# Deform stage of a four-layer convolution kernel: bilinear sides summed by VectorE, and a gathered table of four images

## The chip, the cores and the metric

One core of one Trainium2 chip runs the whole program. The metric is the device time of one execution in microseconds; the median of the runs is given. Engines are named as in the profile: PE is TensorE (its weight loads are listed as PEld), DVE is VectorE, ACT is ScalarE, POOL is GpSimd and SP is SyncE, which only issues DMAs here.

## What is computed

A batch of 32 images of 64 channels and 56 x 56 pixels goes through four residual layers: a hyperbolic two-convolution block, a quantised block, a grouped sign-convolution block, and a deformable 3 x 3 convolution. The change lies in the last one. Cut to what matters:

```python
x = x + _L0_conv_ref(_gn(x), ...)      # stages a_ and b_ of the kernel
x = x + _L1_conv_ref(_gn(x), ...)      # stage c_
x = x + _L2_conv_ref(_gn(x), ...)      # stage d_
x = x + _L3_conv_ref(_gn(x), L3_conv_offset_w, L3_conv_deform_w)   # stage e_

# in the deformable layer, per pixel and tap (9 taps), at a learned fractional position:
p = corner(y0i, x0i, (1 - ly) * (1 - lx))
p = p + corner(y0i, x0i + 1, (1 - ly) * lx)
p = p + corner(y0i + 1, x0i, ly * (1 - lx))
p = p + corner(y0i + 1, x0i + 1, ly * lx)      # then a 64 x 64 matrix per tap
```

`corner` reads the image at integer positions given by data, zero outside of it. So each output pixel needs 9 taps x 4 corners x 64 channels, gathered.

## The kernel before

The stages run one after the other with a barrier between them. Images are worked in pairs (`PAIRS` = 16), 128 partitions holding two images of 64 channels.

**The table.** The deform stage (`deform_phase`) writes each normalised image into a table in DRAM, `k.table`, with `TY` x `TX` = 58 x 59 entries of `ENTRY` = 128 floats. An entry holds a pixel of the row and the one below it, so two neighbouring entries, 256 floats, are the four corners of a tap. The rim has to be zero: the first stage (`l0_conv_phase`, `first`) writes zeros to the table by DMAs from POOL (L496), one for each image of the table, while it computes.

**A tile** is 128 output pixels. There are 49 tiles in a pair (`PX_TILES`), worked in seven groups of seven (`GROUPS`, `SLOTS`); a group is the body `turn(p, group)`, written once for each engine and placed by `around`, which runs the groups of pair p and, between them, the preparations of pair p + 1: after group 0 `normalise`, after 1 `columns` (the table's rows, L1881), after 2 and 3 the offset convolution (`offsets`, L1893), after 4 `turn_offsets` (L1908) and `positions`; after group 6 comes `finish`. All engines follow this one order, each in its own instruction stream.

In a tile the work goes from engine to engine:

- POOL issues nine indirect DMAs (L1779, `gather(slot)`), one for each tap, into `g[:, slot]`. The slot must be free: POOL waits for `bank_done` of the tile that held it, and for `index_ready` from DVE.
- DVE copies the next nine indices (L2015), then multiplies all 2304 gathered values of a pixel with their corner weights in one instruction (L2032). The weights lie in a bank of PSUM, which ACT loads once per group (L1835) when the group before is wholly done.
- PE turns each tap over (pixels to the free side) by a matmul of `g` with the identity, and adds the left and the right side of the four corners in PSUM on the way: two calls per tap (L1922), 18 per tile.
- ACT copies the three banks to `corners` (L1845). PE multiplies with the deform weights, nine calls (L1932), into bank `OUT`, and ACT copies that to `big` (L1850).

A call of `matmul` on 32-bit floats becomes two pairs of weight load and matmul in the trace, so the two lines have 36 and 18 matmuls per tile there.

Of the kernel before, what the change touches and what calls it, by code (L numbers as in the profile page):

```python
# [16 lines left out]
F32 = mybir.dt.float32  # L17
BF16 = mybir.dt.bfloat16
U32 = mybir.dt.uint32
ALU = mybir.AluOpType  # L20
# [26 lines left out]
IMAGE_ENTRIES = TY * TX  # L47
PX_TILES = 2 * HW // P
# [349 lines left out]
def l0_conv_phase(nc, k, first):  # L398
# [8 lines left out]
    with ExitStack() as stack:  # L407
# [50 lines left out]
        with nc.Block() as block:  # L458
# [28 lines left out]
            def _(pool):  # L487
                for t in vpads:
                    pool.memset(t[:, :], 0.0).then_inc(zeroed, 1)
                if first:  # L490
# [1154 lines left out]
def deform_phase(nc, io, k):  # L1645
# [11 lines left out]
    STEPS = 15  # L1657
    with ExitStack() as stack:
# [10 lines left out]
        base, index_base = s.sb("base", [P, 2 * K3]), s.sb("index_base", [P, K3])  # L1669
        w_off, w_def = s.sb("w_off", [P, TAPS * C]), s.sb("w_def", [P, TAPS * C])  # L1670
# [5 lines left out]
        TURN, OUT, PREP, SMALL, WEIGHTS = (0, 1, 2), 3, (4, 5), 6, 7  # L1676
# [8 lines left out]
        (weighted, passed, bank_done, corners_ready, out_done, out_ready) = (  # L1685
            s.sem(n) for n in ("weighted", "passed", "bank_done", "corners_ready", "out_done", "out_ready"))
        (final_v, final_a, x3_used, switched, table_stored, w_loaded) = (
            s.sem(n) for n in ("final_v", "final_a", "x3_used", "switched", "table_stored", "w_loaded"))
        x3_back, stored = ([s.sem(f"{n}{b}") for b in range(2)] for n in ("x3_back", "stored"))
# [24 lines left out]
        with nc.Block() as block:  # L1714
            @block.sync
            def _(sp):
# [3 lines left out]
                def prepare(n):  # L1720
# [18 lines left out]
                    img = n * 2 if isinstance(n, int) else sp.snap(n * 2)  # L1739
# [55 lines left out]
            def _(act):  # L1795
# [35 lines left out]
                def turn(p, group, last=False):  # L1831

                    r = p * GROUPS + group
                    act.wait_ge(weighted, r * SLOTS)
# [28 lines left out]
            def _(pe):  # L1863
# [49 lines left out]
                def turn(p, group, last=False):  # L1913
                    for slot in range(SLOTS):
                        t = p * PX_TILES + group * SLOTS + slot
                        pe.wait_ge(corners_ready, t * 3)
                        pe.wait_ge(weighted, t + 1)
                        for tap in range(TAPS):
                            turned = ps[:, TURN[tap // 4], (tap % 4) * P:(tap % 4 + 1) * P]
                            for side in range(2):  # L1920
                                at_side = tap * CORNERS + side * 2 * C
                                mm = pe.matmul(turned, g[:, slot, at_side:at_side + 2 * C], k.ident[:, :],  # L1922
                                               start=(tap % 4 == 0 and side == 0),
                                               stop=(side == 1), skip_group_check=True)
                            if tap % 4 == 3 or tap == TAPS - 1:
                                mm.then_inc(bank_done, 1)
# [14 lines left out]
            def _(dve):  # L1941
                by_tap = lambda buffer, width: buffer.rearrange("p (n w) -> p n w", w=width)
                dve.wait_ge(const_in, 4 * 16)
# [295 lines left out]
```

## Time and profile before

| | |
|---|---|
| median of 3 runs | 17200.4 us (17161.67 to 17238.65) |
| the profiled execution | 17196.31 us, of which the span of the trace is 17194.7 us |
| PE busy | 11481.5 us (67%) |
| PE weight loads busy | 8617.8 us (50%) |
| POOL busy | 7498.9 us (44%), 7056 indirect DMAs among it |
| DVE busy | 4744.2 us (28%) |
| ACT busy | 3130.7 us (18%) |
| DMA queue of POOL's DMAs | 1020.12 MB, 22.5% of 16 engines' span |
| mean granted TensorE clock | 0.786 of full speed |

No engine is busy all the time, and the stages differ, so the shares of the whole span say little; what is read is the stretch of one stage, which wait ends last in it, and what each engine costs per tile. 784 tiles are worked in the deform stage.

### The profile page before, as it was taken

The numbers are of one execution on the slowest core, as the hardware profiler recorded it, in microseconds if no ns is written. First come the engines' busy times: TensorE is split into PE (matmuls) and PEld (weight loads), VectorE is DVE, ScalarE is ACT, GpSimd is POOL, SyncE is SP. The second block draws the span as 40 slices with busy tenths as digits, with TensorE's granted clock in tenths as the row PEclk, the third lists the DMA queues.
The fourth block names the chain that finished last, engine by engine and source line by source line (L and its number), as shares of the span: only waits on it lengthen the run. The fifth ranks groups of instructions, "written<-read, shape, count | busy, mean of one in ns | idle before, by whom it ended". The sixth has DMA issues, their size and how long they took to land.

```text
span 17194.7 us, 188269 instructions
## 1 busy us (share of the span) xinstructions
PE 11481.5 (67%) x72807; PEld 8617.8 (50%) x72807; DVE 4744.2 (28%) x6831; ACT 3130.7 (18%) x5214; POOL 7498.9 (44%) x7685
## 2 busy tenths in 40 slices
PE   3478788888566666656565657566666666576756
PEld 1133344448455555555555555555555555555555
DVE  3255465553111122121212121212121221212121
ACT  2133344432111111111111111111111111111111
POOL 0001222222455555554555454555455555555455
PEclk7689899999777777777787777777777777787777
DMA  6722111126323233332323232323232332323232
GB/s 103 97 75 83 57 56 56 54 85 184 95 75 99 78 94 85 91 92 77 92 80 92 77 95 78 102 75 103 71 96 77 98 93 81 92 80 97 78 88 75
DMA packets 556369, 1486.74 MB, mean 86 GB/s; under 512 B 174900, under 2 KB 280116, under 8 KB 526992
## 3 DMA queue, kind: packets, MB, share of 16 engines
q0 software_dynamic: 405760, 1020.12, 22.5%
q1 hardware_dynamic: 150032, 458.00, 8.9%
q8 instruction: 475, 7.78, 0.2%
q14 instruction: 102, 0.84, 0.0%
HBM read 1175.46 MB, written 301.96 MB: 86 GB/s over the span
## 4 chain that ended last, share of the span: by engine, by line
PE 43%; issue 18%; another core or an unknown queue 8%; DVE 4%; ACT 1%; DMA 1%; DVEq 0%; ACTq 0%; POOL 0%; SPq 0%
PE e_ps L1922 24%; PE e_ps L1932 11%; PE e_ps L1893 5%; PE e_ps L1908 2%; DVE e_g L2032 2%; PE e_ps L1881 1%; DVE e_sty L2038 1%; DMA out<-e_big 1%; DVE e_w_next L1999 0%; ACT e_corners L1845 0%; DVE e_big L2051 0%; ACT e_ps L1835 0%; DVE e_index_slots L2015 0%; DVE e_tmp L1988 0%
## 5 line engine op out<-in xcount | busy, mean ns | idle before, releaser
L1779 POOL DMA_INDIRECT e_g<-table_dram,e_index_slots x7056 | 6763.3, 959 | 6112.6 <-PE e_ps L1922 2686.4
L1922 PE MATMUL e_ps<-k_ident,e_g 128*128 128x128 f32 x28224 | 4620.1, 319 | 3029.3 <-issue 1805.0
L1922 PEld LDWEIGHTS e_ps<-k_ident,e_g 128*128 128x128 f32 x28224 | 4165.8, 228 | 3500.3 <-issue 2247.7
L1932 PE MATMUL e_ps<-e_corners,e_w_def 128*64 128x128 f32 x14112 | 2316.9, 322 | 1443.0 <-issue 1156.2
L1932 PEld LDWEIGHTS e_ps<-e_corners,e_w_def 128*64 128x64 f32 x14112 | 1901.1, 163 | 1746.6 <-issue 1313.3
L1845 ACT ACTIVATE e_corners<-e_ps 128x512 f32<-128x512 f32 (+1 forms) x2352 | 1119.5, 489 | 5139.6 <-remote 2459.4
L2032 DVE TENSOR_TENSOR e_g<-e_g,e_ps 128x2304 f32<-128x2304 f32 x784 | 1990.0, 2546 | 75.0 <-ACT e_ps L1835 75.0
L2015 DVE COPY e_index_slots<-e_index_now 128x9 uint32<-128x9 uint32 (+1 forms) x784 | 141.0, 181 | 6371.8 <-ACT e_ps L1835 6216.2
L1850 ACT ACTIVATE e_big<-e_ps 64x128 f32<-64x128 f32 (+1 forms) x784 | 212.6, 271 | 4907.3 <-remote 3595.4
L1893 PE MATMUL e_ps<-e_pad,e_w_off 128*64 128x448 f32 x2016 | 794.5, 551 | 32.0 <-issue 30.9
L1197 PE MATMUL c_ps<-c_spad,w_s 128*128 128x448 bf16 x3024 | 614.1, 364 | 7.6 <-ACT c_spad L1069 4.3
L1893 PEld LDWEIGHTS e_ps<-e_pad,e_w_off 128*64 128x64 f32 x2016 | 280.0, 140 | 527.9 <-issue 526.0
L612 PE MATMUL a_ps<-a_vpad,w_w 64*64 64x392 f32 x4608 | 481.7, 546 | 50.5 <-issue 49.6
L612 PE MATMUL b_ps<-b_vpad,w_w 64*64 64x392 f32 x4608 | 458.5, 523 | 25.0 <-issue 24.2
L171 PE MATMUL c_ps<-c_s,k_sel 128*28 128x224 f32 x2240 | 438.5, 355 | 38.3 <-ACT c_s L1012 17.8
L2038 DVE BATCH_NORM_STATS2 e_sty<-e_big 64x6 f32<-64x448 f32 x224 | 119.4, 603 | 1218.7 <-ACT e_big L1850 1143.0
L1197 PEld LDWEIGHTS c_ps<-c_spad,w_s 128*128 128x128 bf16 x3024 | 298.5, 100 | 312.9 <-issue 35.3
L1981 DVE TENSOR_TENSOR e_tmp<-e_ps,e_base 128x450 f32<-128x450 f32 (+1 forms) x32 | 19.8, 618 | 1545.6 <-PE e_ps L1908 1025.7
L1575 PE MATMUL d_ps<-d_spad,w_s 128*128 128x224 bf16 x4032 | 403.0, 261 | 27.0 <-ACT d_spad L1547 23.9
L1575 PEld LDWEIGHTS d_ps<-d_spad,w_s 128*128 128x128 bf16 x4032 | 386.5, 96 | 43.4 <-issue 24.0
L990 POOL TENSOR_TENSOR c_x1t<-c_s,c_xt 128x448 f32<-128x448 f32 x112 | 122.8, 1134 | 559.4 <-DVE c_s L1313 559.4
L1908 PE MATMUL e_ps<-k_ident,e_x3t 18*128 18x18 f32 (+1 forms) x1600 | 329.3, 359 | 55.1 <-issue 54.3
(434 smaller groups left out, 8007.8 us busy)
## 6 DMA issues: line engine op xcount, KB each, us to landing
e_g<-table_dram,e_index_slots POOLq DMA_INDIRECT x7056
table_dram<-a_zeros POOLq DMA_DIRECT2D x32, 1711.0 KB, 90.5
table_dram<-e_rt SPq DMA_DIRECT2D x32, 1624.0 KB
a_xt<-x_in SPq DMA_DIRECT2D x16, 1568.0 KB
v_dram<-a_vout SPq DMA_DIRECT2D x32, 784.0 KB, 8.7
b_xt<-v_dram SPq DMA_DIRECT2D x16, 1568.0 KB
v_dram<-b_vout SPq DMA_DIRECT2D x32, 784.0 KB, 7.3
c_v2t<-v_dram SPq DMA_DIRECT2D x16, 1568.0 KB
```

What stands on the lines that cost most here:

```text
L171: mm = pe.matmul(out, select[:, j, :], source[:, j * SCH:(j + 1) * SCH], start=(j == 0), stop=(j == NS - 1))
L612: mm = pe.matmul(ps[half * C:(half + 1) * C, CONV[2 * (r % 2) + img], 0:RC], w[img * C:(img + 1) * C, tap, :], tile_window(vpads[parity], ...
L1197: mm = pe.matmul(ps[:, CONV[j % 2], 0:CH], parts[n % 3][:, n // 3, :], window(spad[:, :], j, n // 3), start=(n == 0), stop=(n == 3 * TAPS ...
L1575: mm = pe.matmul(ps[:, n % 2, 0:SCH], parts[t % 3][:, t // 3, :], every_other_row(spad[b][:, :], j, t // 3), start=(t == 0), stop=(t == 3 ...
L1779: pool.indirect_dma_start(out=g[:, slot, tap * CORNERS:(tap + 1) * CORNERS], out_offset=None, in_=table, in_offset=bass.IndirectOffsetOnAx ...
L1845: act.activation(corners[:, taps[0]:taps[-1] + 1, :], ps[:, TURN[bank], 0:len(taps) * P].rearrange("p (k x) -> p k x", x=P), ACT.Copy).the ...
L1893: mm = pe.matmul(ps[0:C, PREP[j % 2], 0:CH], w_o[:, tap, :], window(pad[:, :], j, tap), start=(tap == 0), stop=(tap == TAPS - 1))
L1908: mm = pe.matmul(ps[to:to + hi - lo, PREP[half], col * 2 * TAPS:(col + 1) * 2 * TAPS], x3t[rows, lo:hi], k.ident[rows, rows], start=True, ...
L1922: mm = pe.matmul(turned, g[:, slot, at_side:at_side + 2 * C], k.ident[:, :], start=(tap % 4 == 0 and side == 0), stop=(side == 1), skip_gr ...
L1932: mm = pe.matmul(ps[0:C, OUT, 0:P], w_d[:, tap, :], corners[:, tap, :], start=(tap == 0), stop=(tap == TAPS - 1))
L2032: dve.tensor_tensor(tile, tile, w4.unsqueeze(2).broadcast_to([P, TAPS * 4, C]), ALU.mult).then_inc(weighted, 1)
L2038: ins = dve.bn_stats(sty[:, 6 * j:6 * j + 6], big[:, j * CH:(j + 1) * CH])
```

## The change

Two things are changed together.

1. DVE sums the two sides itself. In three batches of taps (4, 4 and 1) it multiplies the right sides into a PSUM bank, `HALF`, multiplies the left sides in place in `g`, waits for both, and adds the bank to `g`. PE then only transposes the sum, one call of `pe.transpose` per tap, batch by batch as DVE finishes them (`added`). The bank for `HALF` is the former `SMALL`; the few values of `SMALL` move to a bank of the preparations.
2. The table holds four images in place of 32; pair p uses half p % 2. The positions are moved between the halves with one more small DVE instruction and a `[128, 1]` buffer. The first stage fills four images with zeros, not 32.

```diff
+TABLE_IMAGES = 4
@@ l0_conv_phase
-                    for b in range(B):
+                    for b in range(TABLE_IMAGES):
                         pool.dma_start(k.table[b]..., zeros...).then_inc(filled, 16)
-                    pool.wait_ge(filled, 16 * B)
+                    pool.wait_ge(filled, 16 * TABLE_IMAGES)
@@ deform_phase, SP
-                    img = n * 2 if isinstance(n, int) else sp.snap(n * 2)
+                    img = n * 2 % TABLE_IMAGES if isinstance(n, int) else sp.snap((n % 2) * 2)
@@ deform_phase, PE
                         pe.wait_ge(corners_ready, t * 3)
-                        pe.wait_ge(weighted, t + 1)
                         for tap in range(TAPS):
-                            turned = ps[:, TURN[tap // 4], (tap % 4) * P:(tap % 4 + 1) * P]
-                            for side in range(2):
-                                at_side = tap * CORNERS + side * 2 * C
-                                mm = pe.matmul(turned, g[:, slot, at_side:at_side + 2 * C], k.ident[:, :],
-                                               start=(tap % 4 == 0 and side == 0),
-                                               stop=(side == 1), skip_group_check=True)
+                            if tap % 4 == 0:
+                                pe.wait_ge(added, t * 3 + (tap // 4 + 1))
+                            mm = pe.transpose(ps[:, TURN[tap // 4], (tap % 4) * P:(tap % 4 + 1) * P],
+                                              g[:, slot, tap * CORNERS:tap * CORNERS + 2 * C], k.ident[:, :])
@@ deform_phase, DVE, positions
-                    c.then(dve.scalar_tensor_tensor(index_next[:, :], flat, float(ENTRY), index_base[:, :],
-                                                    ALU.mult, ALU.add))
-                    c.then(dve.tensor_scalar(index_base[:, :], index_base[:, :],
-                                             float(2 * IMAGE_ENTRIES * ENTRY), None, ALU.add))
+                    c.then(dve.tensor_scalar(flat, flat, float(ENTRY), table_half[:, 0:1], ALU.mult, ALU.add))
+                    c.then(dve.tensor_tensor(index_next[:, :], flat, index_base[:, :], ALU.add))
+                    c.then(dve.tensor_scalar(table_half[:, :], table_half[:, :], -1.0,
+                                             float(2 * IMAGE_ENTRIES * ENTRY), ALU.mult, ALU.add))
@@ deform_phase, DVE, turn
-                        dve.tensor_tensor(tile, tile, w4.unsqueeze(2).broadcast_to([P, TAPS * 4, C]),
-                                          ALU.mult).then_inc(weighted, 1)
+                        for n, (lo, hi) in enumerate(BATCHES):
+                            left = sides[:, lo:hi, 0, :, :]
+                            half = ps[:, HALF, 0:(hi - lo) * 2 * C].rearrange("p (k n c) -> p k n c", n=2, c=C)
+                            need(dve, added, t * 3 + n)
+                            dve.tensor_tensor(half, sides[:, lo:hi, 1, :, :], spread(1), ALU.mult).then_inc(weighted, 1)
+                            dve.tensor_tensor(left, left, spread(0), ALU.mult).then_inc(weighted, 1)
+                            dve.wait_ge(weighted, t * 6 + (2 * n + 2))
+                            dve.tensor_tensor(left, left, half, ALU.add).then_inc(added, 1)
```

On PE, at the start of a group in the deform stage, one tile reads so before the change (each row is a call or a run of equal calls; `e_g` is the gathered tile, `e_ps` the PSUM banks, `k_ident` the identity):

```order
L1916 ISA
L1917 REGISTER_ALU
L1922 MATMUL e_ps<-k_ident,e_g 128x128 x18
L1929 REGISTER_ALU
L1932 MATMUL e_ps<-e_corners,e_w_def 64x128 x4
```

and so after it:

```order
L1921 ISA
L1924 REGISTER_ALU
L1925 MATMUL e_ps<-k_ident,e_g 128x128 x4
L1924 REGISTER_ALU
L1925 MATMUL e_ps<-k_ident,e_g 128x128 x4
L1924 REGISTER_ALU
L1925 MATMUL e_ps<-k_ident,e_g 128x128
L1934 MATMUL e_ps<-e_corners,e_w_def 64x128 x9
```

The 18 calls on the gathered tile became nine, in three runs with a wait value for each; the nine calls with the deform weights are the same.

On DVE, at the start of a group, two tiles read so before the change (the copy is that of the next indices):

```order
L2027 ISA
L2015 COPY e_index_slots<-e_index_now 128x9
L2032 TENSOR_TENSOR e_g<-e_g,e_ps 128x2304
L2015 COPY e_index_slots<-e_index_now 128x9
L2032 TENSOR_TENSOR e_g<-e_g,e_ps 128x2304
```

and the first two batches of one tile read so after it:

```order
L2019 COPY e_index_slots<-e_index_now 128x9
L63 ISA
L2044 TENSOR_TENSOR e_ps<-e_g,e_ps 128x512
L2045 TENSOR_TENSOR e_g<-e_g,e_ps 128x4x128
L2046 ISA
L2047 TENSOR_TENSOR e_g<-e_g,e_ps 128x4x128
L63 REGISTER_ALU
L2044 TENSOR_TENSOR e_ps<-e_g,e_ps 128x512
L2045 TENSOR_TENSOR e_g<-e_g,e_ps 128x4x128
L2046 REGISTER_ALU
L2047 TENSOR_TENSOR e_g<-e_g,e_ps 128x4x128
```

The third batch follows with three instructions on 128 elements. One instruction on 2304 elements became nine, six on 512 elements and three on 128, with a wait on DVE's own results before each first and each third of a batch.

## Rows read from the trace of the kernel before

**Rows 1.** Stretches: start:end, us, busy PE, PEld, DVE, ACT, POOL; PEclk, DMA share, GB/s

```profile
75.00:930.00 855.00, 371.83 (x3622) 151.73 (x3623) 236.96 (x525) 176.60 (x238) 44.01 (x31) 0.70 0.72 100
930.00:1174.00 244.00, 229.98 (x2560) 94.02 (x2562) 152.10 (x338) 113.74 (x158) 0.00 (x0) 0.96 0.30 79
...
4382.00:17128.00 12746.00, 8108.61 (x47128) 6844.46 (x47129) 2647.37 (x2368) 1634.52 (x3641) 6762.81 (x7056) 0.76 0.31 88
```

**Rows 2.** Convolution matmuls of the first stage, L612, 288 per pair, by stretch

```profile
75.00:930.00 855.00, 295.15 (x2680) 103.62 (x2680) 0.70 0.72 100
930.00:1174.00 244.00, 185.89 (x1924) 67.10 (x1928) 0.96 0.30 79
```

**Rows 3.** The zero fill, L496: issues, first and last start, time to landing

```profile
L496 POOL DMA_DIRECT2D table_dram<-a_zeros x32: 1395/2934/4472, 73.3 to 712.3; - x32
...
DMA to landing us min/median/max: 5.4/90.5/219.9
```

**Rows 4.** Waits for the input of the first stage, 0 to 1200 us

```profile
DVE a_st L706 <- DMA a_xt<-x_in: 452.0, 11, 104.3
```

**Rows 5.** POOL's waits, 4382 to 17128 us: total, times, longest

```profile
POOL e_g L1779 <- PE e_ps L1922: 2686.4, 261, 41.5
...
POOL e_g L1779 <- DVE e_index_slots L2015: 867.6, 38, 129.4
POOL e_g L1779 <- remote: 607.9, 373, 7.1
```

**Rows 6.** Groups of instructions, 4382 to 17128 us: busy, mean ns, idle before

```profile
L1779 POOL DMA_INDIRECT e_g<-table_dram,e_index_slots x7056 | 6763.3, 959 | 6112.6 <-PE e_ps L1922 2686.4 <-issue 1950.6 <-DVE e_index_slots L2015 867.6
...
L2032 DVE TENSOR_TENSOR e_g<-e_g,e_ps 128x2304 f32<-128x2304 f32 x781 | 1982.6, 2546 | 75.0 <-ACT e_ps L1835 75.0
```

**Rows 7.** PE in order of time, one group: start, us, last bracket idle before

```profile
9084.95 4.29 PE L1922 MATMUL e_ps<-k_ident,e_g 128*128 128x128 f32 x36
...
9098.70 0.27 PE L1922 MATMUL e_ps<-k_ident,e_g 128*128 128x128 f32 x1 [0.35 <-issue]
9100.09 0.27 PE L1922 MATMUL e_ps<-k_ident,e_g 128*128 128x128 f32 x1 [1.13 <-issue]
...
9109.20 2.28 PE L1922 MATMUL e_ps<-k_ident,e_g 128*128 128x128 f32 x9 [0.32 <-issue]
...
9177.54 6.83 PE L1922 MATMUL e_ps<-k_ident,e_g 128*128 128x128 f32 x36 [11.70 <-issue]
```

**Rows 8.** POOL in order of time, same group

```profile
9083.82 0.95 POOL L1779 DMA_INDIRECT e_g<-table_dram,e_index_slots  x1 [33.07 <-PE e_ps L1922]
...
9105.13 0.95 POOL L1779 DMA_INDIRECT e_g<-table_dram,e_index_slots  x1 [0.30 <-issue]
9112.37 0.95 POOL L1779 DMA_INDIRECT e_g<-table_dram,e_index_slots  x1 [6.30 <-PE e_ps L1922]
```

**Rows 9.** PE in order of time, last group, after the last gather

```profile
17157.00 4.29 PE L1922 MATMUL e_ps<-k_ident,e_g 128*128 128x128 f32 x36
17161.22 2.18 PE L1932 MATMUL e_ps<-e_corners,e_w_def 128*64 128x128 f32 x18
```

**Rows 10.** PE's waits for the first tile of a group, 4382 to 17128 us

```profile
PE e_ps L1922 <- DVE e_g L2032: 1208.1, 108, 43.8
```

**Rows 11.** PE's matmuls of the preparations, 4382 to 17128 us

```profile
L1893 PE MATMUL e_ps<-e_pad,e_w_off 128*64 128x448 f32 x1890 | 746.9, 552 | 31.3 <-issue 30.9
L1908 PE MATMUL e_ps<-k_ident,e_x3t 18*128 18x18 f32 (+1 forms) x1500 | 309.5, 359 | 54.5 <-issue 54.3
...
L1881 PE MATMUL e_ps<-k_ident,e_pad 128*56 128x128 f32 x1680 | 252.7, 322 | 95.3 <-ACT e_rt L1813 53.0 <-issue 42.2
```

**Rows 12.** DVE multiplications on 392 elements with a PSUM input, 75 to 1174 us

```profile
L778 DVE TENSOR_TENSOR a_vpad<-a_ps,a_tile 128x392 f32<-128x392 f32 x128 | 66.6, 562 | 104.7 <-PE a_ps L145 104.3
```

**Rows 13.** A transposition and a matmul, one call each, in the first stage

```profile
L300 PE MATMUL z_ps<-k_ident,z_t x1: 369/369/369, 29.4 to 29.4; 128*1 128x128 f32 x1
L303 PE MATMUL z_ps<-z_max_one,z_one_row x2: 348/358/369, 30.4 to 30.6; 1*128 1x1 f32 x2
```

More of the change, by code:

```diff
@@ L1656, in deform_phase @@
     OFF_ROWS = 32 + 2 * TAPS
-    STEPS = 15
+    STEPS = 16
     with ExitStack() as stack:
@@ L1669, in deform_phase @@
         base, index_base = s.sb("base", [P, 2 * K3]), s.sb("index_base", [P, K3])
+        table_half = s.sb("table_half", [P, 1])
         w_off, w_def = s.sb("w_off", [P, TAPS * C]), s.sb("w_def", [P, TAPS * C])
@@ L1675, in deform_phase @@
         ps = s.ps("ps", [P, 8, 512])
-        TURN, OUT, PREP, SMALL, WEIGHTS = (0, 1, 2), 3, (4, 5), 6, 7
+        TURN, OUT, PREP, HALF, WEIGHTS = (0, 1, 2), 3, (4, 5), 6, 7
+        SMALL = PREP[1]
+        BATCHES = ((0, 4), (4, 8), (8, TAPS))
         padv = pad[:, :].rearrange("p (y x) -> p y x", x=PW)
@@ L1684, in deform_phase @@
                                "coord_step", "index_ready"))
-        (weighted, passed, bank_done, corners_ready, out_done, out_ready) = (
-            s.sem(n) for n in ("weighted", "passed", "bank_done", "corners_ready", "out_done", "out_ready"))
+        (weighted, added, passed, bank_done, corners_ready, out_done, out_ready) = (
+            s.sem(n) for n in ("weighted", "added", "passed", "bank_done", "corners_ready", "out_done", "out_ready"))
         (final_v, final_a, x3_used, switched, table_stored, w_loaded) = (
             s.sem(n) for n in ("final_v", "final_a", "x3_used", "switched", "table_stored", "w_loaded"))
+        half_ready = s.sem("half_ready")
         x3_back, stored = ([s.sem(f"{n}{b}") for b in range(2)] for n in ("x3_back", "stored"))
@@ L1833, in turn @@
                     r = p * GROUPS + group
-                    act.wait_ge(weighted, r * SLOTS)
+                    act.wait_ge(weighted, r * (SLOTS * 6))
                     act.activation(ps[:, WEIGHTS, 0:SLOTS * TAPS * 4],
@@ L1942, in _ @@
                 by_tap = lambda buffer, width: buffer.rearrange("p (n w) -> p n w", w=width)
+                dve.memset(table_half[:, :], 0.0).then_inc(half_ready, 1)
+                dve.wait_ge(half_ready, 1)
                 dve.wait_ge(const_in, 4 * 16)
@@ L2026, in turn @@
                     for slot in range(SLOTS):
+                        t = r * SLOTS + slot
                         dve.wait_ge(gathered[slot], r * (16 * TAPS) + 16 * TAPS)
@@ L2029, in turn @@
                             issue(slot, group * GK + (GK + slot * TAPS))
-                        tile = g[:, slot, :].rearrange("p (n c) -> p n c", c=C)
-                        w4 = ps[:, WEIGHTS, slot * TAPS * 4:(slot + 1) * TAPS * 4]
-                        dve.tensor_tensor(tile, tile, w4.unsqueeze(2).broadcast_to([P, TAPS * 4, C]),
-                                          ALU.mult).then_inc(weighted, 1)
+                        sides = g[:, slot, :].rearrange("p (k s n c) -> p k s n c", s=2, n=2, c=C)
+                        w4 = ps[:, WEIGHTS, slot * TAPS * 4:(slot + 1) * TAPS * 4].rearrange(
+                            "p (k s n) -> p k s n", s=2, n=2)
+                        for n, (lo, hi) in enumerate(BATCHES):
+                            left = sides[:, lo:hi, 0, :, :]
+                            half = ps[:, HALF, 0:(hi - lo) * 2 * C].rearrange("p (k n c) -> p k n c", n=2, c=C)
+                            spread = lambda side: w4[:, lo:hi, side, :].unsqueeze(3).broadcast_to([P, hi - lo, 2, C])
+                            need(dve, added, t * 3 + n)
[3 more added lines that the diff above has]
+                            dve.tensor_tensor(left, left, half, ALU.add).then_inc(added, 1)
                 def finish(p):
```

2 lines of the change are left out of this document (1 added, 1 removed).

## Prediction

> **What bounds the kernel now.** I read the stretches first, then the waits, then PE and POOL in order of time. The deform stage gathers from 4382 to 17128 us [rows 1]: 12,746 us for 16 pairs, 797 us each, or 113.8 us for each of 112 groups. No engine fills it: PE is busy 8109 us, POOL 6763, DVE 2647. POOL needs 0.959 us for an indirect DMA and about 0.305 between two (1950.6 us over 6384 gaps) [rows 6], 11.4 us a tile and 79.7 us a group. The other 34 us of a group POOL waits, mostly for PE to free a slot [rows 5].
>
> Why is PE late? After the last gather a tile costs it 4.29 us on the gathered tile and 2.18 on the deform weights, end to end 6.3 us [rows 9], so seven tiles would take 44 us. While gathers flow it looks different. POOL starts at 9083.82, PE still runs 36 matmuls in 4.29 us at 9084.95, but from 9098.70, 15 us into the flow, matmuls come singly, 1.4 us apart at first; no semaphore is named ("issue"). POOL ends its last gather at 9106.08 and idles 6.3 us, for this very tile; at 9109.20, 3 us later, PE runs again nine at once [rows 7, 8]. I call this a hold. POOL's own stops release PE, and PE's holds bring about the stops. So a group costs POOL's 79.7 us, plus the stops, plus the gap before the next group's first tile, since ACT may load the weights only when PE is through.
>
> The gap is 11.7 us where no preparation lies in it (before 9177.54) [rows 7]. Five boundaries of each pair carry one or the finish: PE's waits for the first multiplication, 1208.1 us [rows 10], and its matmuls of the preparations, 746.9 + 309.5 + 252.7 us [rows 11], are 2517 us over about 79 such boundaries, 31.9 us each.
>
> In the first stage DVE waited 452 us for its input [rows 4] while the 32 fills ran from 73.3 us on, the last issued at 712.3 and up to 219.9 us in flight [rows 3]. Until 930 us there are 2680 convolution matmuls, 9.3 pairs at 92 us; after it 1924 in 244 us, 6.7 pairs at 36.5 us; the DMA share falls from 0.72 to 0.30 [rows 1, 2].
>
> **The change, part by part.** *Fill.* Four of 32 transfers remain, about 855 x 4/32 = 107 us. In those I leave the disturbed pace, 1.2 pairs; the other 8.1 pairs cost 36.5 us each, 297 us. 855 becomes 404, a gain of 451; I take 440, since the first pair has to be loaded and filled in anyway. Bounds: 390 (two more pairs disturbed) to 455.
>
> *Table of four.* A pair still gathers from two images and writes two. Half p % 2 is rewritten by the preparations of pair p + 2, which run a whole pair after its gathers. No wait is added; the small DVE instruction more per pair is well under 1 us, nothing. If addresses within 7 MB or 55 MB mattered, the gathers' landing would show it; POOL does not wait for that, and I take zero.
>
> *DVE per tile.* 2304 elements take 2546 ns [rows 6], 392 take 562 [rows 12]: 1.04 ns an element and 155 ns fixed. So 512 elements take 687 ns and 128 take 288. Six and three are 4.98 us; with the index copy and a small allowance for nine starts with waits, which no row prices (0.3 us), 5.5 us against 2.6. No row shows DVE writing PSUM; if that costs another fixed part each, three times 0.155 makes 6.0, and below nothing speaks for less than 5.0. I take 5.5. Seven tiles are 39 us, under POOL's 80, and DVE does not wait for PE within a group: hidden, unless the holds end.
>
> *PE per tile.* A transposition is one matmul in the trace, another 32-bit call two [rows 13], so the tile goes from 36 + 18 matmuls to 9 + 18, at full speed from 6.3 us to about 3.2 (27 x 0.117), and with the wait for ACT's copies still below DVE's 5.5. PE follows DVE at 5.5 us a tile where nothing holds it.
>
> *The new group, step by step*, with time 0 at PE's first transposition. Slots 0, 1, 2 come free at 6, 11.5 and 17 us, and POOL gathers from 6 on. At 21 us, 15 into the flow, PE is held, with tile 3 half done. In the hold it did nine matmuls in 10.5 us [rows 7], so about 26 in 30 us at best, so by the time POOL has filled slots 0 to 3, at 6 + 4 x 11.4 = 51.6, it has brought through tile 3 but not tile 4's transpositions. POOL stops; 3 us later PE is free, at 56 slot 4 is, POOL resumes, and PE has 15 us again, in which it ends tiles 4, 5 and 6: at 68. Before, the same end lay near 89: the group whose second tile began at 9084.95, the first some 8 us earlier, ended at 9177.54 - 11.70 = 9165.8 [rows 7]. With a gap of 31.9 the next group begins at 99.9. With a short gap POOL is still busy with slots 5 and 6 until 56 + 3 x 11.4 = 90, PE is held again at 71, and the group lasts about 90. A pair is 5 x 99.9 + 2 x 90 = 680 us against 797; 16 pairs gain 1,872.
>
> *Sum.* 17,196 - 440 - 1,872 = 14,884 for the profiled execution's own 17,196; the median stands 4 us above that, which changes nothing. Forecast 14,880. Its own range is 14,300 to 15,600: the group's 68 us may be 62 to 74 (one tile of PE more or fewer before a hold, 112 x 6 = 670).
>
> **Rivals.**
>
> *A. The holds mostly vanish.* For it: they may come from something that PE has half as much of now, such as its instruction stream. Then PE follows DVE, POOL is the bound, and the gaps of 32 us are hidden, because POOL has seven slots (80 us) to fill before it needs the first. 4382 - 440 + 112 x 79.7 + 66 = 12,930 at the least; with loop passes, some holds and the finish, 13,100 to 14,200, say 13,600. Against it: the end of the hold follows POOL's stop, not PE's own progress [rows 7, 8]. Chance 0.27.
>
> A page of the Trainium skill offers such a mechanism: "Runtime: NRT & Kernel Launch", on instruction fetch, says that each engine's stream is refilled by DMA in blocks of 16 KiB (256 instructions), mostly hidden. No row here ties a hold to a block; if one did, half the matmuls would mean half the holds, and A's time.
>
> *B. The holds get longer.* POOL now has more freed slots in front of it when PE is held, so if PE does nearly nothing in a hold, tile 3 waits too and the group ends near 80: 112 x 12 = 1,340 less gain, 16,200. Chance 0.14; between 15,600 and 16,770, where only the fill's 440 would be left.
>
> *C. PE runs at half clock.* The mean was 0.76 [rows 1]; with half the matmuls it may fall to 1.2 GHz for good. 36 matmuls took 6.83 us at 9177.54 and 4.29 at 9084.95 [rows 7], so 0.19 us each and not 0.12; 27 are 5.1 us, with ACT's copies some 6.3 a tile. Each group is then some 5 us longer: 112 x 5 = 560, 15,440. Chance 0.10.
>
> A rule that speaks for C: "TensorE: Matmul & The Clock Gate", part 4, in the Trainium skill, says that transpositions do not count as activity for the clock. No row here shows a run of them.
>
> *D. Slower: DVE is held like PE.* DVE now has ten instructions a tile where it had two, and no row shows DVE working long within a flow of gathers. If each took 1.4 us, as PE's did from 9098.70 on, a tile would take 14 us, seven 98, and with the mean gap of about 25 a group 123: 861 us a pair, +1,020 - 440, 17,780. It decides from 13.5 us a tile on. Against it: POOL's and ACT's instructions keep their pace in the flow (POOL's 0.95 us [rows 8]). Chance 0.05.
>
> *E. Only the fill counts,* POOL and PE settle at the old rhythm: 16,760. Chance 0.04. The forecast has 0.40.
>
> **How the numbers follow.** A change of under 0.5% (86 us) can't be told from none here. Only D and a failed fill lie above: slower 0.05, within 0.01, faster 0.94. The range leaves out the fast end of A (0.06), the slow end of B, E and D (0.14 together): 13,250 to 16,150.
>
> **What the profile will show.** Fill: 4 transfers, DVE's wait for its input under 80 us, the first stage ending near 740 in place of 1174. DVE: nine instructions per tile at 687 and 288 ns; a PSUM write shows in the first of each batch. PE: 9 + 18 matmuls per tile; the line on the gathered tile from 28,224 to 7,056. POOL: 7056 DMAs at 0.959 us, its waits for PE from 2686 us to about 1,000. Holds: singles of the transpositions, mostly in tile 3, ended 3 us after POOL stops. If no singles are left and POOL never waits, A holds. If DVE's instructions stand apart with nothing waited for, D. The forecast is wrong if the 15 us that PE has in a flow depend on something that the change moves, DVE's activity above all.

## The result, and the profile after

The changed kernel took 16286.15 us (median of 4 runs, 16262.03 to 16311.95), the kernel before 17218.46 (4 runs beside it): ratio 0.9464, 95% interval 0.9435 to 0.9492. Faster, but by 932 us and not by the 2,320 forecast, and outside the range. The profiled execution took 16288.56 us, its span is 16286.9 us.

Stretches of the changed kernel, to compare with [rows 1] and [rows 2]: start:end, us, busy time of PE, PEld, DVE, ACT, POOL (instructions), then PEclk, DMA share, GB/s. First the first stage, then the deform stage.

```profile
75.00:719.00 644.00, 566.07 (x6180) 232.91 (x6184) 386.34 (x865) 290.11 (x395) 4.95 (x4) 0.93 0.33 86
3930.00:16220.00 12290.00, 5106.96 (x26109) 3958.54 (x26109) 4371.97 (x8603) 1556.74 (x3638) 6748.50 (x7056) 0.65 0.32 91
```

The fill of the table with zeros did what was forecast. The first stage ends at 719 us and not at 1174, a gain of 455 us (forecast 440). DVE's wait for its input fell from 452 us [rows 4] to 44.6, and four transfers stand where 32 stood [rows 3]:

```profile
DVE a_st L707 <- DMA a_xt<-x_in: 44.6, 4, 21.8
```

```profile
L497 POOL DMA_DIRECT2D table_dram<-a_zeros x4: 1628/2110/2734, 74.0 to 77.2; - x4
```

The deform stage gained as little: its gathers span 12,290 us in place of 12,746, 768 us a pair for 797, where 680 was forecast. Groups of instructions in it (busy us, mean ns, idle before them and what ended it), against [rows 6]:

```profile
L1784 POOL DMA_INDIRECT e_g<-table_dram,e_index_slots x7056 | 6748.5, 956 | 5670.3 <-PE e_ps L1925 2502.9 <-issue 2039.2 <-remote 951.6
L1934 PE MATMUL e_ps<-e_corners,e_w_def 128*64 128x128 f32 x13986 | 2515.5, 353 | 4618.9 <-ACT e_corners L1850 2998.2 <-issue 1590.0
...
L2044 DVE TENSOR_TENSOR e_ps<-e_g,e_ps 128x512 f32<-128x512 f32 (+1 forms) x2331 | 1314.6, 564 | 179.4 <-DVE e_g L2047 96.8 <-issue 25.0 <-remote 5.2
L2047 DVE TENSOR_TENSOR e_g<-e_g,e_ps 128x512 f32<-128x512 f32 (+1 forms) x2331 | 1291.2, 554 | 372.5 <-remote 162.2 <-DVE e_g L2045 82.7 <-issue 53.4
L2045 DVE TENSOR_TENSOR e_g<-e_g,e_ps 128x512 f32<-128x512 f32 (+1 forms) x2331 | 1273.5, 546 | 0.0
L1925 PE MATMUL e_ps<-k_ident,e_g 128*128 128x128 f32 x6993 | 1241.6, 325 | 1879.8 <-DVE e_g L2047 1771.0 <-issue 106.5
```

DVE's nine instructions are as priced, 0.68 to 0.70 us and 0.28 to 0.29, 4.9 us a tile (forecast 5.5), and the one that writes PSUM (L2044) costs no more than the other two. PE's line on the gathered tile is a quarter of what it was. But POOL still waits 2,503 us for PE, hardly less than the 2,686 of [rows 5], and its waits for something without a named releaser ("remote") rose from 608 to 952.

What PE is late with is seen in order of time (start, us; in brackets the idle time before and its releaser). POOL here begins to gather at 9001.9:

```profile
9006.08 2.18 PE L1934 MATMUL e_ps<-e_corners,e_w_def 128*64 128x128 f32 x18
...
9008.19 0.66 PE L1925 MATMUL e_ps<-k_ident,e_g 128*128 128x128 f32 x4
...
9010.37 0.33 PE L1925 MATMUL e_ps<-k_ident,e_g 128*128 128x128 f32 x1 [0.19 <-issue]
...
9021.88 0.94 POOL L1784 DMA_INDIRECT e_g<-table_dram,e_index_slots  x1 [0.30 <-issue]
9023.12 0.95 POOL L1784 DMA_INDIRECT e_g<-table_dram,e_index_slots  x1 [0.30 <-issue]
9027.31 0.27 ACT L1855 ACTIVATE e_big<-e_ps 64x128 f32<-64x128 f32 x1 [20.62 <-remote]
9027.49 1.23 ACT L1850 ACTIVATE e_corners<-e_ps 128x512 f32<-128x512 f32 x3
9028.12 2.18 PE L1934 MATMUL e_ps<-e_corners,e_w_def 128*64 128x128 f32 x9 [17.42 <-ACT e_corners L1850]
9028.32 0.94 POOL L1784 DMA_INDIRECT e_g<-table_dram,e_index_slots  x1 [4.25 <-remote]
```

PE ends its matmuls with the deform weights of one tile at 9008.3 by its record, and the next tile's transpositions at 9010.7. ACT, which waits for just these, starts at 9027.31. Between lies POOL's flow; its last gather ends at 9024.07. The semaphore events of the trace say why. An instruction tells the others that it is done by an increment of a semaphore. PE's four increments (the tile's end and the three banks) arrive together, from 9027.29 to 9027.45, up to 19 us after the matmuls that carry them. DVE worked on through these 17 us at its full pace, though in each batch it waits for increments of its own; those of them that are on record come 0.01 us after their instruction. **In this stretch PE is not slow by its records; its signals come late.** (The start of a matmul is recorded, its end is modelled, so what is seen is that it started in time and that its increment came late.)

I set every increment after 5000 us that is on record against the last instruction of its engine that carries it and had ended, by my own count. `bank_done` tells that a bank of transpositions is done, `out_done` that a tile's last matmul is. Share of PE's increments that come over 2 us late, and the delay that nine in ten stay under:

```
              bank_done        out_done
before      41%,  5.8 us     32%, 15.4 us
after       46%, 16.8 us     60%, 20.1 us
```

Of the increments on record that DVE and ACT give for a tile at most 4% of any semaphore are late. Most signals that come late have no releaser left beside them, so the chain that ended last puts 36% down to an unknown source:

```profile
another core or an unknown queue 36%; PE 19%; issue 12%; DVE 7%; ACT 2%; DMA 1%; ACTq 0%; DVEq 0%; SPq 0%
```

**Not every increment is on record.** After 5000 us the trace of the changed kernel holds 68% of the increments that PE, DVE and ACT give for a tile, and 19,938 of the 112,896 that the landings of the gathers give (7,056 gathers with 16 each); the trace of the kernel before holds 84%, and 30,597. So the shares above are shares of what was recorded. That DVE is not held doesn't rest on them: L2047 waits for DVE's own two increments, and all its idle time is 372.5 us in 2,331 instructions, the longest single wait 3.0 us.

**PE's matmuls come late too, but elsewhere.** Within a tile's run of 36 matmuls on the gathered tile the kernel before waits for nothing. Its trace still has 2,097 steps there of over 0.6 us from one start to the next, where 0.11 is usual, in 199 of the 784 tiles, 2,309 us together beyond it; those of [rows 7] are some of them. In the changed kernel the runs on the gathered tile have none, but the preparations' long runs (L1898 and L1913) have 295 of over 0.5 us beyond the usual step, 478 us together.

### The profile page after: what moved, and what is told of

Its sections match the earlier page's. It is cut to its first block, busy times and chain, and to the rows that moved or that the text cites. A ratio compares the mean times of both kernels' runs of the same rounds, so it can differ in the third digit from the quotient of the medians.

```text
span 16286.9 us, 156056 instructions
## 1 busy us (share of the span) xinstructions
PE 8435.4 (52%) x51639; PEld 5705.0 (35%) x51639; DVE 6489.5 (40%) x13120; ACT 3052.6 (19%) x5214; POOL 7443.3 (46%) x7657
## 4 chain that ended last, share of the span: by engine, by line
another core or an unknown queue 36%; PE 19%; issue 12%; DVE 7%; ACT 2%; DMA 1%; ACTq 0%; DVEq 0%; SPq 0%
PE e_ps L1934 7%; PE e_ps L1898 5%; PE e_ps L1925 2%; PE e_ps L1913 2%; DVE e_g L2045 2%; ACT e_corners L1850 1%; PE e_ps L1886 1%; DVE e_g L2047 1%; DVE e_sty L2052 1%; DMA out<-e_big 1%; DVE e_x3t L1958 1%; DVE e_big L2065 0%; DVE e_w_next L2003 0%; DVE e_x3t L1962 0%
## 5 line engine op out<-in xcount | busy, mean ns | idle before, releaser
L1934 PE MATMUL e_ps<-e_corners,e_w_def 128*64 128x128 f32 x14112 | 2532.7, 352 | 4619.1 <-ACT e_corners L1850 2998.2
L1934 PEld LDWEIGHTS e_ps<-e_corners,e_w_def 128*64 128x64 f32 x14112 | 2215.9, 184 | 4879.8 <-ACT e_corners L1850 3137.4
L1925 PE MATMUL e_ps<-k_ident,e_g 128*128 128x128 f32 x7056 | 1253.4, 325 | 1911.7 <-DVE e_g L2047 1803.0
L1925 PEld LDWEIGHTS e_ps<-k_ident,e_g 128*128 128x128 f32 x7056 | 939.4, 165 | 2223.7 <-DVE e_g L2047 1880.7
L1850 ACT ACTIVATE e_corners<-e_ps 128x512 f32<-128x512 f32 (+1 forms) x2352 | 1041.0, 489 | 2610.4 <-remote 1314.3
L2047 DVE TENSOR_TENSOR e_g<-e_g,e_ps 128x512 f32<-128x512 f32 (+1 forms) x2352 | 1302.8, 554 | 373.3 <-remote 162.2
L2044 DVE TENSOR_TENSOR e_ps<-e_g,e_ps 128x512 f32<-128x512 f32 (+1 forms) x2352 | 1326.4, 564 | 242.9 <-DVE e_g L2047 96.8
L2045 DVE TENSOR_TENSOR e_g<-e_g,e_ps 128x512 f32<-128x512 f32 (+1 forms) x2352 | 1285.0, 546 | 0.0
L1898 PE MATMUL e_ps<-e_pad,e_w_off 128*64 128x448 f32 x2016 | 908.4, 598 | 234.7 <-issue 230.9
L1898 PEld LDWEIGHTS e_ps<-e_pad,e_w_off 128*64 128x64 f32 x2016 | 297.2, 148 | 827.8 <-issue 821.3
L1913 PE MATMUL e_ps<-k_ident,e_x3t 18*128 18x18 f32 (+1 forms) x1600 | 324.3, 344 | 218.1 <-issue 217.3
```

The lines of the kernel that those rows point to most:

```text
L1850: act.activation(corners[:, taps[0]:taps[-1] + 1, :], ps[:, TURN[bank], 0:len(taps) * P].rearrange("p (k x) -> p k x", x=P), ACT.Copy).the ...
L1898: mm = pe.matmul(ps[0:C, PREP[j % 2], 0:CH], w_o[:, tap, :], window(pad[:, :], j, tap), start=(tap == 0), stop=(tap == TAPS - 1))
L1913: mm = pe.matmul(ps[to:to + hi - lo, PREP[half], col * 2 * TAPS:(col + 1) * 2 * TAPS], x3t[rows, lo:hi], k.ident[rows, rows], start=True, ...
L1925: mm = pe.transpose(ps[:, TURN[tap // 4], (tap % 4) * P:(tap % 4 + 1) * P], g[:, slot, tap * CORNERS:tap * CORNERS + 2 * C], k.ident[:, :])
L1934: mm = pe.matmul(ps[0:C, OUT, 0:P], w_d[:, tap, :], corners[:, tap, :], start=(tap == 0), stop=(tap == TAPS - 1))
L2044: dve.tensor_tensor(half, sides[:, lo:hi, 1, :, :], spread(1), ALU.mult).then_inc(weighted, 1)
```

## Experiments

The theory to test, **T**: PE's semaphore increments are held back while POOL's gathers flow at their full rate, and come when the flow pauses. I call a stretch in which they are held back a hold. Rivals: the holds are PE's own (its instruction supply, the pattern of its work), or they go by the bytes that move.

Each set of runs was made on one chip, with the kernel before run in it too. This came to matter: **the same kernel before took 17,180 and 17,224 us in two sets and 13,430, 13,418 and 13,445 us in three**, within 1% inside each set. I call them sets with and without holds; the first comparison (17,218 us) was one with holds. The chip on record has the number 11 in one set with holds and 13 in two without, but number 0 both in a set without holds and, half an hour later, in one with them. If the number names the same chip, the holds are no fixed property of a chip.

**Without gathers** (set with holds). All 7,056 are left out; `g` is zeroed once.

```diff
-                    for tap in range(TAPS):
-                        pool.indirect_dma_start(...).then_inc(gathered[slot], 16)
+                    pool.nop().then_inc(gathered[slot], 16 * TAPS)
```

> The changed kernel with all 7,056 gathers left out (the corner buffers are zeroed once), everything else as it is. Theory 1, TensorE's semaphore signals are held back by the flow of gathers: no hold is left, signals later than 2 us after their matmul fall from 46 and 60% to under 10%, and the stage is bound by VectorE's 4.9 us a tile (35 us a group) and the preparations, some 370 us a pair in place of 774, so about 9,800 us. Rival, the holds are TensorE's own (its instruction supply, or the pattern of its work): they stay, a group stays near 70 us and more, over 560 us a pair, 12,900 us or more.

Measured 10,286 us, 396 us a pair. Of PE's increments 0.3% at most are over 2 us late. The chain that ended last is DVE's now:

```profile
DVE 32%; PE 15%; issue 13%; DMA 2%; ACT 1%; DVEq 0%; ACTq 0%; SPq 0%
```

PE runs the same matmuls in the same order, so its own stream alone doesn't cause the holds. Nor does a supply slowed by the gathers fit: the DMA packets that bring instructions took at most 1.5 us each after 5000 us in the changed kernel with holds, and 1.6 without. T stands. This trace, of a set with holds, also has every increment on record, and no gap in PE's runs.

**Half the bytes** (with holds): only the left 128 floats of each row are gathered, the right side stays zero.

```diff
-                            out=g[:, slot, tap * CORNERS:(tap + 1) * CORNERS], ...
+                            out=g[:, slot, tap * CORNERS:tap * CORNERS + 2 * C], ...
```

> The changed kernel with gathers that bring only the left 128 of the 256 floats of each row, as many gathers and rows as before. What is left out is the right side, which is summed from a buffer zeroed once. If the hold goes by the bytes in flight, it vanishes or shrinks to less than half and the pair falls from 774 to some 600 us, about 13,500 us. If it goes by the number of descriptors (or is TensorE's own), the pair stays at 774 us, 16,290 us within 200.

Measured 16,239 us, ratio to before 0.9452 (0.9407 to 0.9496), as the changed kernel's 0.9464. POOL's instruction is as long, its wait for PE the same (2,458 for 2,503 us), late increments 48 and 59%:

```profile
L1788 POOL DMA_INDIRECT e_g<-table_dram,e_index_slots x7056 | 6755.5, 957 | 5612.7 <-PE e_ps L1929 2457.5
```

Not bytes: what is left is the number of gathers, of their rows or of their increments (16 for each landing) per time. No run separates these.

**Spaced gathers** (with holds): a memset of 256 bytes a partition behind each gather.

```diff
                         ).then_inc(gathered[slot], 16)
+                        pool.memset(pace[:, tap * 256:(tap + 1) * 256], 0).then_inc(paced, 1)
...
+                        pool.wait_ge(paced, r * GK + slot * TAPS)
                         pause(pool, index_ready, r * SLOTS + (slot + 1), passed)
```

> The changed kernel with a small memset of some 0.28 us on GpSimd behind each gather, so that they start every 1.55 us or so and not every 1.25. Theory 1, holds come of gathers at the full rate: they vanish or become rare, GpSimd's group is 63 x 1.55 = 98 us and sets the pace, 700 to 730 us a pair, 15,100 to 15,600 us. Rival, holds don't depend on the rate: they stay as long, and GpSimd's 18 us more a group come on top, 17,000 us or more.

Measured 14,919 us, ratio 0.8684 (0.8657 to 0.8710), under the range expected, since gathers start 1.447 us apart and not 1.55, and 2.17 between tiles (the wait for the last memset). POOL now does more and the kernel is 1,370 us faster than the changed one. Of the increments on record (88%) 0.3% at most are late, POOL's waits for PE fell from 2,503 us to

```profile
POOL e_g L1786 <- PE e_ps L1931: 1.6, 10, 0.2
```

and the chain that ended last is POOL's:

```profile
POOL 59%; issue 12%; PE 2%; DVE 1%; POOLq 1%; DMA 0%; ACT 0%; DVEq 0%; SPq 0%; ACTq 0%
```

**A pause at each tile** (with holds): POOL waits for the tile's gathers to land.

```diff
                         gather(slot)
+                        pool.wait_ge(gathered[slot], r * (16 * TAPS) + 16 * TAPS)
```

> The changed kernel in which GpSimd, behind the nine gathers of a tile, waits until they have landed before it goes on to the next tile: a pause of some 2 us every 11.3 us. Theory 1, a pause in the flow releases what TensorE has signalled: each tile's signals come within one tile, PE is late by at most some 13 us, GpSimd's group is 80 + 7 x 2 = 94 us and sets the pace, some 670 to 700 us a pair, 14,600 to 15,100 us. Rival, the holds are not of the flow: the pauses only come on top of the stops, 16,500 to 17,500 us.

Measured 15,246 us, ratio 0.8879 (0.8851 to 0.8908), above the range expected. Gathers are 1.25 us apart within a tile and 3.68 us between tiles, one pause longer than I had put in. Late increments: 4% (`bank_done`) and 20% (`out_done`, 99 in 100 of them within 5.8 us). So a hold begins within one tile of gathers and such a pause ends most of them.

**Shorter gaps.** One memset a tile in place of nine, and a memset of 16 in place of 256 behind each gather. Both were first run in sets without holds:

```diff
+                        if tap % 9 == 8:
                             pool.memset(pace[:, tap * 256:(tap + 1) * 256], 0).then_inc(paced, 1)
```

> The changed kernel with one memset of 256 columns (0.33 us, as in the paced kernel) behind each ninth gather only, once a tile. If a gap of this length lets out what TensorE has signalled, signals come within a tile (late by at most 11 us), GpSimd's group is 80 + 2 = 82 us and the pair some 590 to 640 us, 13,300 to 14,000 us. If it is the mean rate that counts, the rate is nearly unchanged, holds stay, and the time is 16,250 to 16,500 us.

> The changed kernel with a shorter memset (16 in place of 256 columns, some 0.12 us) on GpSimd behind each gather, so that they start every 1.4 us or so: 63 x 1.4 = 88 us a group, and a hold of TensorE's signals is then a matter of whether this is slow enough. If any slowing or any gap between gathers is enough, no hold, some 630 to 650 us a pair and 13,900 to 14,300 us. If the rate must fall to something near the 1.6 us of the paced kernel, holds are back for some or all of the time: 15,500 us or more.

They took 13,738 and 13,565 us, where before took 13,430: slower than before (ratios 1.0235 and 1.0109), with no signal held. A repeat of the first,

> The changed kernel with one memset of 0.33 us and the wait for the last one between tiles, so gathers start every 1.25 us within a tile and once after 2.2 us between tiles; where no signal was held it took 13,738 us, 612 us a pair. Theory: one such gap a tile lets out what TensorE has signalled, so that on a chip with holds too the time is 13,700 to 14,300 us. Rival, the mean rate counts or the gap must be near the 3.6 us of the kernel that waits for landing (709 us a pair there): 15,000 to 16,400 us.

gave 13,733 where before took 13,418. The missing holds look like the memsets' doing until the time of the kernel before in the same set is seen: they are missing there too. Then with holds:

> The kernel with one memset a tile again, for a chip on which the kernel before takes 17,200 us (twice it was run where before takes 13,430 us, and took 13,735). If the one gap of 2.2 us between the gathers of two tiles lets the signals out, 13,700 to 14,300 us. If the rate within a tile (1.25 us) starts a hold that so short a gap doesn't end, 15,000 to 16,400 us.

> The kernel with the short memset behind each gather again, for a chip on which before takes 17,200 us (13,565 us where it takes 13,430). Its gathers start every 1.26 us within a tile, as without memsets, and 1.96 us apart between tiles. If what ends a hold is time without a gather, this gap is the shortest of the three and it is at or above the kernel with one memset a tile: 15,500 to 16,400 us. If work of another kind between gathers on GpSimd is enough, 13,600 to 14,000 us.

Measured 15,845 and 15,973 us (ratios 0.9207 and 0.9278): 52 to 61% of increments late, and POOL still waits 1,755 and 1,916 us for PE (2,503 in the changed kernel). The short memset fits into the 0.30 us between two gathers; they stay 1.257 us apart within a tile, so work between them doesn't end the holds; nor does a gap of 2.2 us once a tile.

**Between 1.25 and 1.45 us** (the first with holds, the second without), memsets of 160 and 128:

> The changed kernel with a memset of 160 columns behind each gather: gathers some 1.35 us apart, between the 1.26 us of the short memset and the 1.45 us of the long one, with which no signal was held. GpSimd alone would set 90 us a group, some 635 us a pair, 14,050 to 14,200 us on either kind of chip, if 1.35 us is slow enough. If it isn't, 15,500 us or more on a chip with holds.

> The changed kernel with a memset of 128 columns behind each gather: gathers some 1.33 us apart, between 1.26 us (holds to 15 us and more, 15,973 us) and 1.36 us (holds to 5 us, 14,335 us). If the hold grows steadily as the interval shrinks, holds of 5 to 10 us and a time set by GpSimd still, 14,100 to 14,300 us. If there is an edge between the two, GpSimd stops again and it is over 14,500 us.

The first: 14,335 us, ratio to before 0.8328 (0.8297 to 0.8358), the fastest of all with holds and 12% under the changed kernel. Gathers are 1.363 us apart; 37% of PE's increments are late, but 99 in 100 come within 6.6 us, and POOL's waits for PE are 2 us in all. The second took 14,173 us at 1.340 us apart; where it ran no signal is ever held, so it says nothing of the limit.

In one table (intervals in us, pairs and the share of late increments among those on record, from the traces, by my own count):

```
with holds             gathers apart   between   late bank_/out_done  us a pair   us
changed kernel              1.251        1.25+        46% / 60%          774    16,286
16 behind each              1.257        1.96+        52% / 61%          757    15,973
256, once a tile            1.251        2.2+         56% / 56%          746    15,845
wait for landing            1.250        3.7           4% / 20%          709    15,246
256 behind each             1.447        2.17          0% / 0%           686    14,919
160 behind each             1.363        2.08         37% / 37%, short   649    14,335
without holds: changed      1.251        1.25          0% / 0%           564    12,969
```

**What differs between the sets in the traces** is how much of the increments they hold. Of the 112,896 of the gathers' landings, the eight traces of gathering kernels with holds have 17 to 69% (changed kernel 18%, 16 behind each 17%, once a tile 22%, 160 behind each 35%, 256 behind each 69%), the eleven from sets without holds 99.5% and more. Of the engines' increments for a tile it is 64 to 88%, against all of them. Every execution timed here has a granted clock on record, so all were traced. **A rival of all that is said of T was therefore never tested: that recording the increments, with 16 for each gather, is itself what holds PE's signals in some sets.** It would fit the run without gathers, half the bytes, and the spaced gathers as well as T does. That the two go together is shown; which is the cause isn't, nor whether an execution that isn't traced has holds at all.

**The changed kernel again, and its two parts alone** (without holds). The first part alone is the kernel before with the table of four and the new positions, the second the changed kernel with `TABLE_IMAGES` and the positions as before:

> The changed kernel unchanged, beside the kernel before on the same chip, since the kernel before took 13,430 us on one of the chips and 17,200 us on the others. On a chip where before takes some 17,200 us: 16,290 us again, signals of TensorE held. On a chip where it takes some 13,430 us, with no held signal: both deform stages are set by GpSimd's 80 us a group (before's pair there is (13,430 - 4,450) / 16 = 561 us), so only the fill's 455 us is left: 12,950 to 13,050 us. If VectorE's sums were a gain by themselves there, less than that.

> The kernel before with the four-image table alone; TensorE still sums the sides. The fill is worth the 455 us measured in the two traces on any chip: 16,750 us where before takes 17,200 us, 12,975 us where before takes 13,430 us. If in a chip with holds a shift of the start changed the pattern of holds, more than 100 us off.

> The changed kernel with the table of all 32 images; VectorE sums the sides. By the two traces the stage gained 456 us of 12,951 from the sums: 16,740 us where before takes 17,200 us. Where before takes 13,430 us and GpSimd sets the pace already: no gain, 13,400 to 13,500 us, or a loss if VectorE's signals, later than TensorE's old ones, lengthen GpSimd's waits.

Against before's 13,418 us: changed 12,969, ratio 0.9669 (0.9653 to 0.9686); four-image table alone 12,972, ratio 0.9672 (0.9655 to 0.9688); VectorE's sums alone 13,426, ratio 0.9997 (0.9987 to 1.0007). All the gain is the fill's, the sums give nothing. POOL never waits for PE there, with the sums (first) or without (second, four-image table alone, TensorE summing):

```profile
POOL e_g L1784 <- issue: 2093.3, 6872, 0.3
POOL e_g L1784 <- PE e_ps L1925: 51.2, 168, 0.3
```

```profile
POOL e_g L1782 <- issue: 2119.8, 6953, 0.3
POOL e_g L1782 <- PE e_ps L1925: 26.8, 88, 0.3
```

The longest wait is 0.3 us, the usual space between two gathers. Both parts were run once more,

> The four-image table alone again, for a chip on which before takes 17,200 us: the fill's 455 us and nothing else, 16,750 to 16,800 us. If the start of the stage shifts the pattern of holds, more than 100 us off. (12,972 us was measured where before takes 13,430 us.)

> VectorE's sums alone with the 32-image table, for a chip on which before takes 17,200 us: 456 us by the two traces, from the 32 us a pair by which GpSimd's stops are shorter, so 16,700 to 16,800 us. (13,426 us, no gain, was measured where before takes 13,430 us.)

again in a set without holds: 12,989 and 13,442 beside 13,445. What each is worth alone under holds was not measured; the two traces with holds put 455 us in the first stage and 456 in the deform stage.

**Before, with spaced gathers** (both without holds), the same edit with memsets of 256 and 160 in the kernel before:

> The kernel before (TensorE sums the sides, 32-image table) with the memset of 256 columns behind each gather. If the stage of both kernels is set by the held signals and with pacing by GpSimd alone, both paced kernels have the same deform stage, and this one is slower than the paced changed kernel by the fill's 455 us: 15,300 to 15,500 us. If TensorE's nine extra matmuls a tile are on the path when no signal is held, it is 15,700 us or more. If the stops before were not of the held signals, pacing makes it slower than 17,200 us.

> The kernel before with the memset of 160 columns behind each gather, for a chip on which before takes 17,200 us. If VectorE's sums are worth nothing once holds are short, 14,335 + 455 = 14,790 us. If TensorE's nine extra matmuls a tile, with holds of up to 5 us in a tile time of 13 us, make GpSimd stop, 15,000 us or more.

15,330 and 14,789 us, which is 411 and 454 us above the changed kernel with the same memsets (14,919 and 14,335, with holds): close to the fill's 455, and nothing for the sums, even with signals up to 6 us late on the other side. The comparison goes across sets. Whether PE's sums would do as well under such holds was not run.

## Why the forecast was wrong

- **Fill:** right; 455 for 440.
- **DVE per tile:** 4.9 us for 5.5; PSUM as an output costs nothing extra (L2044 0.70 us, L2045 0.68). Seven tiles lie under POOL's 80 us a group. Right.
- **PE per tile:** free tiles took 3.3 to 3.6 us from the first transposition to the last matmul, for 3.2. Right.
- **PE's time in a group:** forecast 497 us a pair without the gaps, by the working (680 less 5 x 31.9 and 2 x 11.7). Measured 531 (pairs 3 to 14). The scheme gave PE 15 us in each flow, after which it is held in tile 3 (from 0). The signals are late far sooner. Of the signals of matmuls that end 6 to 10 us into a flow 93 to 95% come over 2 us late in the changed kernel, and 89 to 92% in the kernel before; of those in the first 4 us 7 and 1% (a flow is gathers with no pause of over 1 us between them). The 15 us were read from the first single matmul of [rows 7], but in that same group the signal of a bank done at 9088.79, 5 us into the flow, comes 3.5 us late, and that of a tile done at 9094.80 comes 14.4 us late, at 9109.22. So in most groups of the changed kernel tile 2 takes 23.5 us, and tile 4 again 20, with a stop of POOL at each. In each pair's second group tile 1 takes 42 us.
- **The gap before the next group: the step that failed most.** It was carried over, "With a gap of 31.9 the next group begins at 99.9", as if it lay outside the holds. The seven gaps of a pair were 183 us before and are 243 after, 60 x 16 = 960 us of the missing 1,416 (1,872 less the 456 between the two spans). The last signal of a group is now held, so ACT loads the weights late and DVE starts late: ACT's copy of the group's last tile starts some 20 us after PE's record of it ends in the last five groups of a pair (median), where it was 0 to 2 us before. The 34 us a pair inside the groups are 540 more (pairs 3 to 14 take 774 us, all of them 768 in the mean, so the two terms come to a little too much).
- **What a hold is.** "In the hold it did nine matmuls in 10.5 us" took it for late matmuls alone, so that fewer matmuls get through sooner. Late matmuls are real in the kernel before (the 2,309 us of gaps), and the change took most of it away. But the increments are late as well, and every tile needs a round trip from PE to ACT and back, so a tile with half the matmuls waits as long. Here the forecast argued from the records of matmuls alone. The increments of before, 41 and 32% of them over 2 us late, lay in the trace and would have told it. Why PE's long runs have gaps in a hold stays open.
- **Rivals.** B (holds longer, 16,200) came nearest in time, and partly in kind: a held tile waits however few its matmuls are, tiles 2 and 4 where B had tile 3. But the group's PE time grew less than its gap. A's argument (instruction supply) fell with the run without gathers; its time, 12,930 at the least, is that of a set without holds (12,969), where the kernel before too loses its stops, so that it comes near is luck. Nothing here ties a hold to what the page cited there, "Runtime: NRT & Kernel Launch" of the Trainium skill, says of instruction fetch: the run without gathers fetches PE's same instructions and has no hold. C: the mean granted clock of the stage fell from 0.76 to 0.65, but a free tile of 3.3 to 3.6 us isn't what anything waits for, and with spaced gathers POOL sets the pace at a mean clock of 0.73; not at work. In sets without holds the clock is lower with the sums as well (0.71 for 0.85, four-image table in both, 4000 to 12900 us), and the two kernels take the same time. Whether the rule of "TensorE: Matmul & The Clock Gate" in the Trainium skill that is cited beside C or the fewer matmuls lower it, no run separates. D: DVE kept 0.69 us in the flow; fell. E (only the fill counts, 16,760) is what happened in the sets without holds: 449 us, and nothing for the sums.
- "The forecast is wrong if the 15 us that PE has in a flow depend on something that the change moves": there were no such 15 us for PE's signals, before or after.

## What to carry to other kernels

When an engine waits for one that seems done, compare semaphore events with the ends of the instructions, engine by engine, before pricing its work: a late signal isn't cured by less work. Count the events first: where a third of them is missing, the recording itself is a suspect, and a gain found under it may not be there in an execution without a trace. If signals are late only while one stream of DMAs is issued at full rate, try to space that stream: in the sets with holds 0.11 us more between gathers, and 0.8 between tiles, took 1,950 us off. And run the kernel before in each set: what looked like the effect of an edit was once that of the set. Spacing that gains 12% with holds (at 1.363 us apart) costs 9% without (14,173 for 12,969 us, at 1.340 us apart).

## What the runs showed of the hardware

- While indirect DMAs of 128 rows were issued every 1.25 us, PE's increments came late (one in a hundred by over 36 us in the changed kernel). Of those over 10 us late 97 in 100 arrived while POOL paused in the kernel before and 91 in the changed one, half of them 3.1 to 3.4 us after its last gather ended; of those over 2 us late a third arrived within a flow. DVE's and ACT's on record hardly ever came late. At 1.363 us apart 99 in 100 of PE's came within 6.6 us, at 1.447 within 1.4. Halving the bytes changed nothing.
- It happened in three sets of runs and not in three others, with the same kernels. Gathers' instructions were as long in both (0.956 and 0.972 us), the first gather came at 3931 and 3921 us, DVE's sums took the same time. What differs is the share of the increments that the traces hold (18% of the landings' in the changed kernel with holds, 99.8% without). The mechanism, and whether holds exist without a trace, stays open.
- In the sets without holds GpSimd, not TensorE, sets the pace of this stage: 63 gathers x 1.25 us are 79 us a group, 553 us a pair, and 564 us were measured.
